# Token regions at fixed places per expert, routing in groups of 512 tokens, and results gathered ahead of the attention

## What is computed

```python
scores = sigmoid(x @ gate_w);  idx = top_k(scores + bias, 2)
w = scores[idx] / sum(scores[idx])
out = sum over the 2 experts of w * (silu(x @ W1[e]) * (x @ W3[e])) @ W2[e]
out = out + shared expert(x);   x = x + 0.5 * out
```

## Time and profile before

| | us |
|---|---|
| median of three runs | 1083.51 (1081.23 to 1085.17) |
| the profiled execution | 1087.36 |
| its span, first to last instruction | 1085.5 |
| outside its span | 1.86 |
| busy in the span: PE, DVE, ACT, POOL | 814.8, 468.2, 370.5, 360.0 |
| mean granted TensorE clock | 0.88 |

### The profile page before, as it was taken

One profiled execution on the slowest core, in us unless ns is written; L12 is line 12 of the kernel. 1 busy time (PEld: TensorE's weight loads), 2 busy tenths in 40 slices (PEclk: granted clock), 3 DMA queues, 4 the chain that ended last, 5 costly groups with the idle time before them and its releaser, 6 DMA issues.

```text
span 1085.5 us, 13666 instructions
## 1 busy us (share of the span) xinstructions
PE 814.8 (75%) x3674; PEld 546.9 (50%) x3675; DVE 468.2 (43%) x1388; ACT 370.5 (34%) x1012; POOL 360.0 (33%) x378
## 2 busy tenths in 40 slices
PE   5966999917997948999737459962699968349990
PEld 2333777703563426777513248851477743228870
DVE  4712222247565603322275522226666674612224
ACT  3200133335534100333243015544365533005552
POOL 0371033350000660233341745545000000744555
PEclk9987999967998979999959669995899989759995
DMA  8941133150000121233290234425000000234438
GB/s 286 314 150 63 44 108 107 64 174 0 1 1 1 63 92 40 90 105 95 81 357 15 87 126 149 152 89 149 1 1 1 1 0 1 83 120 143 151 106 242
DMA packets 79775, 104.54 MB, mean 96 GB/s; under 512 B 10422, under 2 KB 68150, under 8 KB 79158
## 3 DMA queue, kind: packets, MB, share of 16 engines
q1 hardware_dynamic: 65318, 64.51, 19.5%
q0 software_dynamic: 14400, 39.34, 10.2%
HBM read 56.23 MB, written 47.58 MB: 96 GB/s over the span
## 4 chain that ended last, share of the span: by engine, by line
PE 65%; DVE 11%; issue 8%; ACT 5%; DMA 4%; SPq 3%; another core or an unknown queue 2%; POOL 1%; DVEq 0%; ACTq 0%
PE bank L804 16%; PE bank L823 10%; PE bank L717 8%; PE bank L728 6%; PE bank L860 4%; PE bank L779 3%; PE bank L704 3%; PE bank L813 3%; PE bank L911 3%; DMA XT<-f_result_rows 2%; PE bank L685 2%; SPq L393 2%; PE bank L945 2%; PE bank L972 2%; ACT XT L472 2%
## 5 line engine op out<-in xcount | busy, mean ns | idle before, releaser
L413 POOL DMA_INDIRECT f_result_rows<-arena x172 | 164.8, 958 | 290.2 <-ACT arena L524 267.3
L413 POOL DMA_INDIRECT slot_rows<-XN,slots x128 | 139.0, 1086 | 313.5 <-DVE slots L1146 275.7
L804 PE MATMUL bank<-w,arena 128*128 x688 | 203.6, 418 | 6.9 <-issue 4.7
L1243 DVE COPY arena<-bank 88x128 f32<-88x128 f32 (+1 forms) x250 | 65.2, 285 | 243.5 <-PE bank L813 228.0
L804 PEld LDWEIGHTS bank<-w,arena 128*128 128x128 f32 x688 | 129.2, 190 | 41.2 <-issue 11.7
L823 PE MATMUL bank<-w,arena 88*128 (+1 forms) x500 | 136.5, 381 | 0.0
L728 PE MATMUL bank<-f_s,arena 128*128 128x256 f32 (+1 forms) x256 | 75.4, 449 | 69.8 <-DVE X L1201 46.5
L717 PE MATMUL bank<-XT,f_s 128*128 128x512 f32 (+1 forms) x256 | 120.9, 626 | 8.5 <-issue 6.1
L685 PE MATMUL bank<-ident,XN 128*128 128x128 f32 x192 | 40.9, 329 | 111.7 <-DVE XN L1064 97.0
L511 ACT ACTIVATE arena<-bank 128x256 f32<-128x256 f32 x172 | 65.8, 384 | 101.7 <-PE bank L779 100.9
L728 PEld LDWEIGHTS bank<-f_s,arena 128*128 128x128 f32 (+1 forms) x256 | 54.1, 221 | 92.1 <-DVE X L1201 51.0
(11 more groups left out here) (133 smaller groups left out, 1043.1 us busy)
## 6 DMA issues: line engine op xcount, KB each, us to landing
arena<-slot_rows SPq DMA_DIRECT2D x172, 128.0 KB
XN<-f_result_rows SPq DMA_DIRECT2D x16, 512.0 KB, 6.0
XT<-f_result_rows SPq DMA_DIRECT2D x32, 256.0 KB, 6.4
slot_rows<-zeros SPq DMA_DIRECT2D x1, 6016.0 KB, 20.2
w<-in_f_w SPq DMA_DIRECT2D x1, 4096.0 KB, 14.8
w<-in_f_w SPq DMA_DIRECT2D x1, 2816.0 KB
f_result_rows<-arena POOLq DMA_INDIRECT x172
X<-in_x SPq DMA_DIRECT2D x4, 512.0 KB, 5.1
```

The costliest lines, as they stand in the source:

```text
L413: pool.indirect_dma_start(out=dst, out_offset=bass.IndirectOffsetOnAxis(ap=idx, axis=0), in_=src, in_offset=None).then_inc(done.sem, 16)
L804: last = pe.matmul(bank[2 + q % 2][:, 0:2 * m.H], xsT[q % 2][:, k, :], L["w13"][:, k, bass.ds(e, 1), :], start=(k == 0), stop=(k == KD - 1))
L1243: last = dve.tensor_copy(hT[q % 2][0:kp, k, :], bank[4 + q % 2][0:kp, k * P:(k + 1) * P])
```

## The change

It gives each expert a fixed region of 2176 rows in the DRAM buffer, so that a token's row needs only the running count of its expert. The routing is done for 512 tokens at a time: `choose(g)` and `place(g)` on DVE (13 and 7 instructions on 64 or 32 columns in place of 256 or 128), `positions(g)` on PE, 8 scatters on POOL for each group. The running counts go from group to group in `f_carry`. Normalising moves from DVE to ACT in all stages but h (`Identity` with scale and bias), and the transposes use one PSUM bank. The router matmuls have 32 output rows and go to four quarters of one bank. Shared-expert pieces (two a group in f0, one in f1) stand between the groups. ACT's order in a group is normalise, four copies, logits copy, sigmoid, silu, stdev of the next group, in f0 a second silu.

`tile_lists` makes the tiles' experts and first rows (`f_start`); SP zeroes the 128 rows behind each expert's last one and loads row tiles from addresses in registers. Without gathers (three of the four mixtures) `close_slots`, `split_slots`, `mark` and `slot_tokens` follow between and behind the shared adds, and PE waits for `rows` before its first expert tile.

In the f1 stage ahead of the attention nothing of that is needed: POOL stores each result tile in order and later gathers both rows of each token, eight indirect DMAs a group, groups 1 to 3 while the attention runs. There the attention takes groups 1, 2 and 3 in (combine, moments, scales on DVE; stdev, normalise and copies on ACT; transposes on PE) in steps 0 and 1, 2 and 3, 4 and 5. POOL adds the output bias. The attention's loop is written out. In the other stages the second results land in Y2 as whole rows; DVE does both additions of `combine`, 8 instructions a group, and a stage starts when its first group is there. The recurrence transposes group g+1 behind the last pieces of `project(g)`. The 6 MB fill of zeros at the start is gone.

```diff
+SPACE = 2048 + P
+                for g in range(NG):
+                    pool.wait_ge(*s["slotted"](g + 1))
+                    for i in range(GT * g, GT * (g + 1)):
+                        for k in range(2):
+                            scatter(x_rows, slots[:, k, i:i + 1], XN[:, i, :], s["rows_out"])
+                if s["gathers"]:
+                    pool.wait_ge(*s["closed"](1))
+                    for q in range(R):
+                        pool.wait_ge(*s["y_out"][q](16 * turns(tiles, q)))
...
+                    for g in range(NG):
+                        for i in range(GT * g, GT * (g + 1)):
+                            gather(XN[:, i, :], y_slots, closed_slots[:, 0, i:i + 1], s["y_got"][g])
+                            gather(Y2[:, i, :], y_slots, closed_slots[:, 1, i:i + 1], s["y_got"][g])
+                        if g:
+                            plus_bias(g - 1)
...
 ACT, mixture:
-                for g in range(NG):
-                    weight(s["prev"], g)
-                stdev(s, 0)
-                stdev(s, 1)
-                for g in range(NG):
-                    for t in range(GT):
-                        copy_xT(s, g, t)
-                    if g + 2 < NG:
-                        stdev(s, g + 2)
-                    logits(g)
-                act.wait_ge(*s["lg_psum"](NG))
+                stdev(s, 0)
                 for g in range(NG):
+                    normalise(s, g)
+                    for t in range(GT):
+                        copy_xT(s, g, t, banks=1)
                     logits(g)
+                    score(g)
+                    shared_silu(per * g)
+                    if g + 1 < NG:
+                        stdev(s, g + 1)
+                    if per > 1:
+                        shared_silu(per * g + 1)
...
 PE, mixture:
+                loaded(pe, s["kind"] + "_shared")
                 for g in range(NG):
+                    if g:
+                        positions(g - 1)
                     for t in range(GT):
-                        transpose_x(s, g, t)
+                        transpose_x(s, g, t, banks=1)
                     logits(g)
+                    logits_back(g)
+                    for n in range(per * g, per * (g + 1)):
+                        shared_up(n)
+                positions(NG - 1)
+                if nk > 1:
+                    shared_up(per * NG)
                 shared_down(0)
+                for n in range(per * NG + 1, NG * nk):
+                    shared_up(n)
                 for g in range(1, NG):
                     shared_down(g)
+                if not s["gathers"]:
+                    slot_tokens()
...
+                if not s["gathers"]:
+                    pe.wait_ge(*s["rows"](1))
                 xT(0, 0, 0)
...
 DVE, mixture:
+                for g in range(NG):
+                    taken(s, g)
+                    moments(s, g)
+                    if g:
+                        choose(g - 1)
+                    scales(s, g)
+                    if g:
+                        place(g - 1)
+                        shared_hidden(per * (g - 1), per * g)
+                choose(NG - 1)
+                place(NG - 1)
+                shared_hidden(per * (NG - 1), per * NG)
+                tile_lists()
                 shared_add(0)
+                if not s["gathers"]:
+                    close_slots()
+                    split_slots()
+                    mark(0)
...
+                shared_add(1)
+                if not s["gathers"]:
+                    mark(1)
+                for g in range(2, NG):
                     shared_add(g)
+                if not s["gathers"]:
+                    rows()
...
 PE, recurrence:
-                            if g < 2 and k < 2:
-                                transpose_x(s, g + 2, 2 * c + k, banks=1)
+                            if g + 1 < NG and c and k:
+                                transpose_x(s, g + 1, 2 * k - 2, banks=1)
+                                transpose_x(s, g + 1, 2 * k - 1, banks=1)
```

More of the change, by code:

```diff
@@ new lines, in _, with starts @@
+                for e in range(E):
+                    sp.dma_start(x_rows[bass.ds(ends[e], P), :], zeros[:, :]).then_inc(s["filled"].sem, 16)
+                def starts(j, n):
+                    _, held["rows"] = nc.values_load_multi_w_load_instructions(
+                        f_start[0:1, bass.ds(j, n)], engines=(mybir.EngineType.SP,), min_val=0,
+                        max_val=E * SPACE - P,
+                        skip_runtime_bounds_check_because="the vector engine has limited them to the regions")
+                    held["first"] = j if known(j) else R - 2
@@ L1252, in mixture @@
                 rounds(dve, NT, step, more=1)
+                if s["gathers"]:
+                    close_slots()
+                weights()
+                assert steps[0] == ROUTE_STEPS[s["gathers"]], steps
             def recurrence(s):
```

594 lines of the change are left out of this document (310 added, 284 removed).

## The result

The changed kernel takes 1125.84 us (median of 4 runs, 1123.87 to 1131.32), the kernel before 1082.6 beside it: ratio 1.0405, 95% interval 1.036 to 1.045. It is 43 us slower, where I had forecast 3 us faster and a range up to 1112. The profiled execution took 1131.32 us, its span is 1129.5.

What follows compares the result with a forecast made beforehand. PE was taken as full in the expert loop and settled attention, so only the ways between could move, set by one group's time; terms 0+0-3-9+9+3-3 sum to -3, giving 1080.5 us, range 1048 to 1112.

Steps and rivals of the forecast that it cites:

- The group's turn: Mixtures' group loop: one group of 512 tokens takes 16 us in f0 (14.9 to 18), 15.3 in f1 (13.5 to 17).
- Rival 2: Group loop: ACT's round with PE at the low clock takes 18 and 17 us a group; 28 more, 1108; chance 0.17.
- rival 4: New group loop: the slow stretch returns, PE's issue slow beside any scatters; twice 14 us, 1108; chance 0.04.
- First and second f0: Both f0 stages up to their experts: no change, ranges -4 to +6 and -6 to +10 us.
- slow stretch beside the scatters: Second f0: 14 us of slow PE beside back-to-back scatters is won, and the group loop's pace gives it back.
- h: Recurrence stage: begins 12.5 us earlier, transposes inside add 9.5; -3 us in all, range -10 to +4.
- First f1: First f1 to its experts: -9 us; starts 7 earlier, then takes 82; range -16 to 0.
- Last f1: Last f1 to its experts: DVE's serial line is the bound, 97.6 against 89.0 us; +9, range +1 to +17.
- Attention: Attention: first maxima 14 us earlier, three arriving groups cost 5.5 each, 17 in all; +3, range -10 to +13.
- rival 3: Attention: DVE's and ACT's blocks add up fully, 9 us a group; 1091; chance 0.06.
- End: End of the kernel: read-back as long, last additions 3.3 us in place of 9.9; -3, range -5 to 0.
- The rule on table loads: ACT's table switches: each costs a 1.38 us drain beside the 1.28 load; 13 us in all, 1093; chance 0.04.

Runs made afterwards that it cites:

- set 2: Runs on a chip where the kernel before takes 1083.31 us; the changed kernel, unedited, took 1127.29 us there (ratio 1.0407).
- set 3: Runs on a chip where the kernel before takes 1047.68 us; the changed kernel, unedited, took 1103.06 us there (ratio 1.0538).
- version without gathers: Changed kernel with DVE normalisation, two transpose banks, low marks by groups, results by rows everywhere, all groups prepared ahead of attention: 1022.63 us (0.9772); slower chip 1052.11 (0.9696).
- Sigmoid version: Changed kernel with DVE normalisation and two transpose banks, plus Sigmoid in place of Silu in the mixtures' shared pieces: 1075.23 us.
- low marks by groups: Changed kernel with DVE normalisation and two transpose banks, plus marks of the slot's low seven bits made inside the group loop: 1065.71 us.
- the run meant to tell it: Changed kernel with scatters held back until all four groups have slots, repeated on a faster chip: 1171.03 us.
- version with both edits: Changed kernel with the mixtures' normalisation on DVE and two banks for the transposed tiles: 1069.00 us (ratio 0.9874); again 1067.02 (0.9857).

## Why the prediction was wrong, step by step

**The group's turn** failed, and it is the largest miss: I took 16 us in f0 and 15.3 in f1 with bounds of 18 and 17. Measured in the profiled execution are 17.5, 17.7 and 19.1 in the second f0, 16.0 to 17.4 in the f1 stages. Its terms in the turn of 17.7: normalise, copies and transposes 5.35 (forecast 5.3); router 2.7 (1.1); logits, transpose and hops 0.6 (0.8); two shared pieces 8.4 (7.0); silu and hop 0.6 (0.7). Two terms failed. I priced the shared pieces with a row of a full stretch, where they run at the full clock; in this loop PE idles for a third of each turn, the granted clock is 0.80, and the price is 1.4 more. The router's matmuls take the 1.08 that I had for them (0.64 at clock 1.00; the 0.85 worked out beside it lies between the two), but their result takes 1.6 us longer than that to reach ACT here. Rival 2 had the clock's part of this, with 18 and 17 us, 1108 us and 0.17 of the chance. It should have been the likeliest case: my own sum left PE waiting in every turn, and the one row of a PE that waits showed 0.64. I priced the copies between the two clocks and the shared pieces, the largest term, at the full one. Of the router's late result rival 4 had something (PE slower beside any scatters, 0.04 of the chance): it adds up to 15 us over twelve groups, and its cause is open.

**First and second f0 (0 and 0; +10.5 and +10.8).** Of the second's 10.8, three turns are 6.3 and the rest, fourth group and shared remainder, 4.9. The wait for the shared weights in the first f0, for which I had named up to 5 us, is there: PE begins 6.1 us after the normalisation in place of 0.75 in the second f0, and what it waited for is `f_s`.

```profile
16.42 0.66 PE L734 MATMUL bank<-ident,XN 128*128 128x128 f32 x2 [16.42 <-DMA f_s<-in_f_s]
```

That both stages miss alike is luck: from there on the first is 3.0 us shorter than the second. The slow stretch beside the scatters was won, as predicted (behind the group loop PE has no gap over 2.6 us in the second f0), and given back with 10 us on top.

**h (-3; -0.5).** Right in both halves: the first projection comes 11.3 us earlier relative to the experts before it (forecast 12.5), and the stage is 10.8 longer inside (9.5).

**First f1 (-9; -5.0).** The start comes 7.2 earlier (7), the way from there takes 86.3 (82), by the turn again.

**Last f1 (+9; +14.4).** DVE's serial line was right: from the last normalisation 50.6 us against 49.1. The three turns are 50.4 against 45.9.

**Attention (+3; +13.1).** The earlier start was right (16.7; forecast 14). The arrivals cost 9.9 each where I took 5.5 out of 1 to 9: outside my bounds, and a little more than rival 3's 9. The failed step is the slack: DVE and ACT, busy for 52 and 45 of 82 us, seemed to have 2 to 3 us free in a half step, and I took it off both of their blocks, 5.0 and 6.6 us. What the runs show is that hardly anything comes off: without the two table loads of 2.6 us an arrival is 2.3 shorter. That each of the two engines is a link of one chain (scores, maxima, exponentials, weights, transposes) is the reason that I give for it, argued and not shown.

**End (-3; +0.8).** Read-back and last additions are 2.5 shorter (24.7 against 27.2 from the last result's scatter to the end), as forecast. The expert loop ahead of it is 3.3 longer, from 82.8 to 86.1; no run explains that.

**The rule on table loads.** ACT's switches cost 1.28 each and rose from 18 to 70. A load starts 0.02 us after the instruction ahead of it has ended, with no drain between (364.39 and 364.61 in the timeline of a group above). By the Trainium skill (ScalarE: Activation LUTs, What ACT_TABLE_LOAD costs) such a switch has a drain of 1.38 us on top of the load; here no drain shows. By the Trainium skill (ScalarE: Activation LUTs, Table sets: the hidden batching unit) activations are to be batched by set; here the trace agrees for the attention alone: without 18 of the loads the mixtures gain nothing, without the square root's the attention gains 2.3 for each arrival.

Summed up: the four mixtures miss by 10.5, 10.8, 4.0 and 5.4, 31 us together, the attention by 10, h and the end by 6: 47 us between the forecast sum of -3 and the span's +44.

## What to carry to other kernels

When work is cut into groups so that one engine can begin earlier, write down one turn and count who waits for whom in it: a normalisation that stands behind the last activation of the group before makes two engines take turns. Moving it to a third engine or giving the transposes a second bank was worth 38 us each on one kind of chip, where the cut had lost 55, and the two together 58 on the other, where it had lost 44. Price a matrix product by the clock of the stretch in which it will stand, from a row with waits like its own: the two shared pieces of a turn, priced at 7.0 us from a full stretch, took 8.4. Work put into a stretch that is already full costs more than the same work ahead of it, even where each engine's busy share leaves room.

## What the runs showed of the hardware

Fillers that nobody reads made the kernel 17.6 us faster: 18 more transpositions a group, granted clock from 0.75 to 0.87 over three turns of the second f0.

On the chips where the kernel before takes 1083 us, the router's result reaches ACT 1.15 us after the start of its matmuls in the first group of each mixture of the changed kernel, and after 1.5 to 2.8 us in the other twelve, which have scatters beside them. Where the kernel before takes 1047, it is 1.15 in all sixteen. ACT's copy of the result in the third group of the second f0, of the changed kernel in set 2 and in set 3:

```profile
379.95 0.28 ACT L525 ACTIVATE arena<-bank 128x128 f32<-128x128 f32 x1 [2.62 <-PE bank L753]
```

```profile
372.14 0.28 ACT L525 ACTIVATE arena<-bank 128x128 f32<-128x128 f32 x1 [1.20 <-PE bank L753]
```

The twelve late results add up to 15 us, beside 24 us between 1127 and 1103. With the shorter turns of the version without gathers the scatters follow each other closely, and on the slower kind of chip one group of the second f0 stalls outright, until 3 us after the last scatter beside it (PE's router matmuls, then ACT's copy):

```profile
346.05 1.08 PE L744 MATMUL bank<-XT,f_router 128*32 128x128 f32 x16 [3.06 <-issue]
...
352.79 0.28 ACT L516 ACTIVATE arena<-bank 128x128 f32<-128x128 f32 x1 [6.79 <-remote]
```

Two more profiles on this kind, of the Sigmoid version and of the low marks by groups, have one such group (6.7 and 8.1 us). On the faster kind 32 scatters in a row pass there without it. That the scatters are the cause is argued from where the late results stand, not shown: the run meant to tell it came on a chip of the faster kind. Scatters beside a group are not enough: in the version with both edits, on the slower kind, nine of the twelve later groups have the result after 0.9 to 1.15 us with scatters beside them too, and only three have it late. Whether PE issues late or its signal is late stays open, and so does what differs between the chips.
